# One burst of identity transposes in place of three, and two handovers made per token block

## The reference

```
i, f, g = x @ Wi.T, x @ Wf.T, x @ Wg.T
h[t] = sigmoid(f[t]) * h[t-1] + silu(i[t]) * (1 - sigmoid(f[t]))
xg = h * silu(g)
x1 = layernorm(x + (xg * rsqrt(mean(xg^2) + eps) * w_norm) @ Wo)
x2 = layernorm(x1 + wkv(w, u, keys=x1, values=ctx))     # a recurrence over the tokens
x3 = layernorm(x2 + int8_mlp(x2))                       # quantised per token and per weight row
```

## Time and profile before

| | |
|---|---|
| median of 3 runs | 420.44 us (419.89 to 420.63) |
| time of the profiled execution | 419.63 us |
| its span, first to last instruction | 417.7 us |
| PE busy | 370.7 us (89%) |
| DVE busy | 362.9 us (87%) |
| ACT busy | 320.9 us (77%) |
| POOL busy | 232.9 us (56%) |
| mean granted TensorE clock | 0.983 of full speed |

### The profile page before, as it was taken

One profiled execution on the slowest core, in us unless ns is written; L12 is line 12 of the kernel. 1 busy time (PEld: TensorE's weight loads), 2 busy tenths in 40 slices (PEclk: granted clock), 3 DMA queues, 4 the chain that ended last, 5 costly groups with the idle time before them and its releaser, 6 DMA issues.

```text
span 417.7 us, 7901 instructions
## 1 busy us (share of the span) xinstructions
PE 370.7 (89%) x2756; PEld 290.5 (70%) x2778; DVE 362.9 (87%) x620; ACT 320.9 (77%) x422; POOL 232.9 (56%) x274
## 2 busy tenths in 40 slices
PE   7798899989898899999999999999999998486872
PEld 7797798769775778678866977597759774233331
DVE  3889899869677899989998999899989999998684
ACT  3778599597927899599958996899679976985671
POOL 1574573843526656674667557664767554645451
PEclk9999999999999999999999999999999999888997
DMA  7978356010200020301011020202030202000101
GB/s 246 369 262 322 101 192 240 0 52 27 102 1 2 0 77 1 116 14 50 27 55 73 10 69 25 102 0 75 0 126 0 75 0 75 25 1 2 50 27 51
DMA packets 12842, 31.74 MB, mean 76 GB/s; under 512 B 2038, under 2 KB 5132, under 8 KB 12812
## 3 DMA queue, kind: packets, MB, share of 16 engines
q1 hardware_dynamic: 12812, 31.35, 21.5%
HBM read 27.14 MB, written 4.21 MB: 75 GB/s over the span
## 4 chain that ended last, share of the span: by engine, by line
DVE 26%; PE 24%; ACT 17%; issue 14%; POOL 14%; DMA 2%; SPq 1%; DVEq 0%; POOLq 0%; ACTq 0%
PE proj_ps L502 14%; PE slot_ps L607 6%; POOL den L1269 5%; ACT L1009 3%; DVE hid_top L1648 2%; DVE stats L1584 2%; ACT hqT L974 2%; DVE inp L1487 2%; POOL ring L1294 2%; DVE num L1577 2%; DVE ring L1629 2%; DMA ring<-w_gate_up_dram 2%; DVE x_max L1603 2%; DVE ring L1632 2%; POOL late L1299 2%
## 5 line engine op out<-in xcount | busy, mean ns | idle before, releaser
L1294 POOL TENSOR_TENSOR ring<-ring 128x512 f32<-128x512 f32 (+1 forms) x48 | 62.4, 1302 | 41.2 <-ACT ring L960 41.2
L607 PE MATMUL slot_ps<-w1q,xqT 128*128 128x512 bf16 (+1 forms) x377 | 80.0, 361 | 5.7 <-ACT xqT L951 2.9
L607 PEld LDWEIGHTS slot_ps<-w1q,xqT 128*128 128x128 bf16 x384 | 35.9, 98 | 44.6 <-issue 3.3
L502 PE MATMUL proj_ps<-x_high,proj_high 128*128 128x256 f32 x384 | 64.8, 290 | 0.9 <-ACT proj_high L887 0.5
L502 PE MATMUL proj_ps<-x_low,proj_high 128*128 128x256 f32 x384 | 61.6, 282 | 0.0
L502 PE MATMUL proj_ps<-x_high,proj_low 128*128 128x256 f32 x384 | 61.5, 282 | 0.0
L502 PEld LDWEIGHTS proj_ps<-x_high,proj_high 128*128 128x128 f32 x384 | 53.1, 189 | 2.9 <-issue 0.7
L502 PEld LDWEIGHTS proj_ps<-x_high,proj_low 128*128 128x128 f32 x384 | 52.7, 189 | 0.0
L502 PEld LDWEIGHTS proj_ps<-x_low,proj_high 128*128 128x128 f32 x384 | 52.4, 188 | 0.0
L960 ACT ACTIVATE ring<-ring,zero_bias,x_scale 128x512 f32<-128x512 f32 (+1 forms) x48 | 36.8, 771 | 15.6 <-DVE ring L1629 15.6
L1269 POOL TENSOR_TENSOR den<-den,q_state 128x512 f32<-128x512 f32 x16 | 28.1, 1771 | 35.2 <-ACT q_state L920 35.2
(11 more groups left out here) (146 smaller groups left out, 824.7 us busy)
## 6 DMA issues: line engine op xcount, KB each, us to landing
ring<-w_gate_up_dram SPq DMA_DIRECT2D x11, 512.0 KB, 4.4
forget<-xT_dram SPq DMA_DIRECT2D x8, 512.0 KB, 3.8
x_sb<-x_dram SPq DMA_DIRECT2D x8, 512.0 KB, 3.5
c_sb<-cT_dram SPq DMA_DIRECT2D x8, 512.0 KB, 4.4
out_dram<-late SPq DMA_DIRECT2D x16, 256.0 KB, 2.1
late<-w_down_dram SPq DMA_DIRECT2D x2, 704.0 KB, 6.7
ring<-w_down_dram SPq DMA_DIRECT2D x2, 704.0 KB, 4.4
scale_rows<-scratch_dram SPq DMA_DIRECT2D x2, 704.0 KB, 6.1
```

Of the source, the lines that this page charges most:

```text
L502: last = nc.tensor.matmul(out, a, b, start=(i == 0), stop=(i == len(terms) - 1))
L607: last = nc.tensor.matmul(slot_ps[:, s, half * 512:half * 512 + width], xqT[:, par, d, t * P:(t + 1) * P], w1q[:, d, half * I + at:half * ...
L1294: nc.gpsimd.tensor_tensor(hid, hid, gate_buf[:, at:at + width], ALU.mult).then_inc(hid_ready, 1)
```

## The change

In PE's prologue the three bursts and their three waits are replaced by one wait for `mlp_read` at 3 and one burst of 32 transposes; they write another place in PSUM. `split_states` subtracts one token block at a time, each with its own increment of `xg_low_ready`, and `project_out(b, t)` waits for its own block. `turn_inputs` goes through the token blocks in its outer loop and waits for `x2_rounded` of each block; it issues the same 8 transposes. The last two edits hold for every batch.

```diff
@@ project_out
                 pe.wait_ge(xg_high_ready, b + 1)
-                pe.wait_ge(xg_low_ready, b + 1)
+                pe.wait_ge(xg_low_ready, b * TB + t + 1)
@@ turn_inputs
-                pe.wait_ge(x2_rounded, 2 * b + 2)
                 pe.wait_ge(z2_ready, 2 * b + 2)
-                for c in range(DB):
-                    for t in range(TB):
+                for t in range(TB):
+                    pe.wait_ge(x2_rounded, 2 * b + t + 1)
+                    for c in range(DB):
                         last = nc.tensor.transpose(turn_16[:, c, t * P:(t + 1) * P],
                                                    low_halves(z2[:, t, c * P:(c + 1) * P]),
                                                    identity16[:, :])
@@ PE's list, prologue
             project(2, 5)
-            pe.wait_ge(proj_read, 2 * PROJ + 5)
-            keep_busy(28, proj_ps[:, 0, 0:P // 2])
-            pe.wait_ge(num_ready, 4)
-            keep_busy(36, proj_ps[:, 0, 0:P // 2])
-            pe.wait_ge(h_ready, 3)
-            keep_busy(28, proj_ps[:, 0, 0:P // 2])
+            pe.wait_ge(mlp_read, 3)
+            keep_busy(32)
             turn_values(1, 0)
@@ split_states on DVE
                 dve.wait_ge(xg_high_ready, b + 1)
-                nc.vector.tensor_tensor(flat(xg_low), flat(inp), flat(xg_high).bitcast(F32),
-                                        ALU.subtract).then_inc(xg_low_ready, 1)
+                for t in range(TB):
+                    tok = slice(t * P, (t + 1) * P)
+                    nc.vector.tensor_tensor(xg_low[:, :, tok], inp[:, :, tok],
+                                            xg_high[:, :, tok].bitcast(F32),
+                                            ALU.subtract).then_inc(xg_low_ready, 1)
```

## The result

The kernel after takes 418.22 us (median of 7 runs, 417.13 to 419.14), the kernel before on the same chip 420.70 (7 runs, 419.89 to 423.44). The ratio is 0.9921, 95% interval 0.9897 to 0.9946: faster by 3.3 us, between 2.3 and 4.3. The two medians themselves lie 2.5 us apart, which is inside that interval. 417.6 was forecast. Each interval here leaves out runs more than 1.5% above the fastest of their kernel, one of them a run of 750.10 us among the 12 of the kernel before that e5 to e8 are compared with.

What follows compares the result with a forecast made beforehand. No engine is full (PE 89%, DVE 87%), so the chain of waits decides, with late filler on it. Terms -3.26 + 0.25 + 0.45 + 0.05 - 0.35 = -2.86 from 420.44 give 417.6 us, range 415.8 to 418.7.

Steps and rivals of the forecast that it cites:

- The burst, -3.26: PE's prologue: 32 transposes end before refine's release, so hidden_max_row(0, 0) starts 3.26 us earlier, at 115.6.
- Batch 1, +0.45: Prologue: POOL's round_rows(12) steps between the halves of split_states(1), the second ends 1.5 us later, 0.45 reaches the chain.
- the lower bound of 0.05: Batch 1 in the prologue: the cost is only 0.05 us if DVE keeps its turn for both halves.
- `split_states` in the iterations, +0.25: Two DVE instructions of 0.6 us for one at 1.15 cost 0.05 us a batch, 0.25 over five.
- rival D: Slower: POOL's pair_squares steps between the split_states halves every iteration, +3.6 us, 424.0; chance 0.04.
- Batch 0, +0.05: split_states of batch 0, now in two halves, costs 0.05 us.
- `turn_inputs`, -0.35: Iterations: fewer transposes after the last round_2, but x1 limits the gain to 0.07 us on average, 0.35 over five.
- the bound of 1.15: Largest gain allowed for turn_inputs: the full 0.23 us in each of five iterations, 1.15 us.
- B: Engines don't take turns as read and x1 is no limit: -4.6 us, 415.9, or 416.7 with half the difference; chance 0.25.
- C: Most of the gain is hidden by another prologue wait late after 115: 419.7 us; chance 0.07.
- that the change doesn't do what it says: In PE's prologue, mlp_read is met later than read from the trace; no size given; chance 0.02.
- E: Slower: 60 transposes fewer let the granted clock fall after 110, 425.8 us; chance 0.04.

Runs made afterwards that it cites:

- e5: The kernel after without the burst of 32 and its wait: 418.28 us, 0.9931 of the kernel before.
- e8: The kernel after, with DVE in batch 1 alone waiting for its own first half of split_states before the second: 418.43 us, one run.
- e3: The kernel before with only split_states and its wait by token block: 421.31 us, 0.9992 of the kernel before.
- e4: The kernel before with only turn_inputs by token block: 419.05 us, 0.9924 of the kernel before.
- e1: The kernel before with only the new burst (wait for mlp_read at 3, 32 transposes): 418.17 us, 0.9913 of the kernel before.
- e12: The kernel after with an unused two-input POOL product added ahead of round_rows(12): 416.37 us, one run.
- e7: The kernel after with layer_norm_2(1) put ahead of split_states(2) and hidden_max_row(0, 0) on DVE: 417.16 us, 0.9914 of the kernel before.
- e11: The kernel after with DVE order layer_norm_2(1), first half of split_states(2), hidden_max_row(0, 0), second half: 415.21 us, 0.9839 of the kernel before.

## Why the prediction was right

The forecast was 417.6 and the measurement 418.22; the interval of the difference (-2.3 to -4.3) holds the -2.86 of the sum. Its terms did not all hold, and that it came so close to the medians (2.5 apart) is partly luck: the stages give -4.0, and the runs can't tell the two apart.

- **The burst, -3.26: right, by its own steps.** 32 transposes end ahead of `refine`, `residual_2` follows `gating(2)`, and POOL's third product is what is late next, lengthened to 1.5 us. Measured: -3.31. The third MLP chunk was forecast for 122.1 after waiting 1.6 us for DVE. It starts at 125.39, which is 122.1 and the 3.3 by which this execution is late, and waits 1.15. That the new wait holds nothing up is right too: the burst stands directly behind `project(2, 5)`.
- **Batch 1, +0.45: wrong.** The step that failed is "POOL gets its turn between two DVE instructions in a row". It had been read from a POOL product with two inputs and was carried over to a scaling with one. `normalise_2(0)` came 10.11 us after `gating(1)`, before 10.13. What happened is what the lower bound of 0.05 stands for: DVE keeps its turn for both halves.
- **`split_states` in the iterations, +0.25: right,** +0.27 (e3). All 16 halves on line 1490, by duration in ns (least, median, most), show that POOL never came between those of the iterations, which was rival D:

```profile
L1490 DVE TENSOR_TENSOR xg_low<-inp,xg_high x16: 673/684/692, 39.0 to 338.9; 128x512 fp32r<-128x512 f32 x16
```

- **Batch 0, +0.05:** +0.08, within the scatter: e4, which leaves `split_states` alone, shows +0.05 in the same stage.
- **`turn_inputs`, -0.35: right in its mechanism, mis-sized by a factor of three.** Measured -1.05 (e4), close to the bound of 1.15. In e4 every iteration is shorter by 0.19 to 0.23, iteration 1 included. The prediction let x1 stop the gain there, as x1 stood behind the load of x^T: "that path does not move". The rows after the change, to be set against the earlier trace rows:

```profile
174.63 0.38 PE L580 MATMUL turn_ps<-identity,num 128*128 128x128 f16 x4 [0.51 <-ACT num L940]
...
175.25 0.40 PE L580 MATMUL turn_ps<-identity,num 128*128 128x128 f16 x4 [0.23 <-ACT num L940]
...
175.68 1.11 ACT L947 ACTIVATE xqT<-turn_ps,half_bias 128x1024 bf16<-128x1024 f16 x1 [0.49 <-PE turn_ps L580]
...
177.18 1.15 ACT L862 ACTIVATE x_high<-forget,zero_bias 128x1024 fp32r<-128x1024 f32 x1 [0.38 <-DMA forget<-xT_dram]
178.23 1.51 ACT L928 ACTIVATE x<-inp,shift,rstd 128x512 f32<-128x512 f32 x2
...
180.40 1.04 PE L560 MATMUL turn_ps<-identity,x 128*128 128x128 f32 x8
```

  x1 is ready at 179.74, 0.61 earlier than before, because the load took 3.3 us from issue to landing and not 4.1. That was a matter of the execution: in e1 and e3, where `turn_inputs` is as before, ACT doesn't wait for this load at all. Nor did x1 hold `turn_keys` up. Counted from ACT's read of `xqT`, x1 is ready after 4.54 us in the profile before, 3.79 in e1, 3.73 in e3 and 4.06 after the change; the transposes of `turn_keys` start after 4.78, 4.72, 4.71 and 4.72. So they start when PE is through with the first two chunks of `mlp_up`, and the late x1 of the one profile before cost them 0.06. First PE's row of the kernel before, then e1's timelines:

```profile
180.59 1.06 PE L560 MATMUL turn_ps<-identity,x 128*128 128x128 f32 x8
```
```profile
173.28 1.11 ACT L947 ACTIVATE xqT<-turn_ps,half_bias 128x1024 bf16<-128x1024 f16 x1 [0.71 <-PE turn_ps L580]
174.51 1.15 ACT L862 ACTIVATE x_high<-forget,zero_bias 128x1024 fp32r<-128x1024 f32 x1
175.56 1.51 ACT L928 ACTIVATE x<-inp,shift,rstd 128x512 f32<-128x512 f32 x2
```
```profile
178.00 1.04 PE L560 MATMUL turn_ps<-identity,x 128*128 128x128 f32 x8
```

  The prediction took a distance of 0.21 us between x1 and the weight load, seen in one execution, for a dependence that limits.

The two wrong terms, +0.45 and -0.35, missed on the same side, by 0.45 and 0.70; with them put right the sum is -4.0, as the stages have it. The forecast stood because the burst's term, the largest, was right.

Of the rivals, B was half right (x1 was no limit) and half wrong (the engines do take turns: 1.52 at 117.33). C is refuted by the stage's -3.31, D by the halves above, and that the change doesn't do what it says by the burst's place. E, the lower clock after 110, did not occur in the profile after the change (1.00 from 110 to 118). It occurred in e4, with all the old bursts in place: the filler behind the pause did not prevent it.

## What to carry to other kernels

Filler on an in-order queue is free only up to the moment at which its successor could start: compare its end with the release of the next instruction, and place it before the pause, not behind the wait that ends the pause. Whether it is needed at all is a question of its own; here one profile without it kept the clock. When a wait is taken away, look at what is late next and at the order of that engine's list. Here one reordering on DVE gave another 1.4 us. And compare stages that repeat from execution to execution where totals spread by more than the effect looked for. A limit read from one execution is checked against a second one: here one slow load passed for the limit of an iteration.

## What the runs showed of the hardware

- A POOL instruction that meets two DVE subtractions back to back steps in between them if it multiplies two SBUF tensors (POOL 1.60 in e12 and 1.68 in e7, the DVE pair 2.37 and 2.35 instead of 1.27). If it scales one tensor by a column it waits for both (2.33, the pair 1.27; with 512 elements 2.64), unless DVE pauses for a semaphore between them (1.83, the pair 2.55). Between a scan and a DVE instruction with two tensors and a column the scaling steps in too (2.75, DVE 1.11 instead of 0.74). The Trainium skill (SBUF — State Buffer, section "SBUF: two separate sides") speaks of an exclusive lock on the shared ports. That one engine waits while the other runs agrees with all of these; which engine gets its turn next, these runs alone show.
- The same pause of PE, behind the same code, lowers the granted clock in one execution and not in another. Ahead of the old bursts, 1.95 us: 0.51 to 0.64 in e4, 1.00 in the kernel before. In the first 20 us, 2.04 in e5: down to 0.50; 2.00 in the kernel before: 1.00. Near 47 us, 1.81: 0.64 to 0.80 from 46 to 52 in e8 and e11, 1.00 after the change; the stage from `gating(0)` to `gating(1)` took 1.6 longer in these two. And 2.40 in e5, ahead of `turn_values`: 1.00. For e5, PE's timeline and a window:

```profile
18.21 0.62 PE L661 MATMUL slot_ps<-identity,ring 128*128 128x128 f16 x8 [2.04 <-POOL ring L1224]
```
```profile
20.00:22.00 2.00, 2.00 (x12) 2.00 (x11) 1.74 (x4) 2.00 (x3) 1.48 (x2) 0.50 0.93 305
```

- The start also depends on when weights land. After the change ACT waited 3.15 us for the weights of i, and PE 3.78 behind it:

```profile
16.32 1.15 ACT L883 ACTIVATE proj_high<-den,zero_bias 128x1024 fp32r<-128x1024 f32 x1 [3.15 <-DMA den<-wiT_dram]
```

  The change touches nothing there, and in the kernel before ACT's step began at 14.89. Late weights and the lower clock together put `gating(0)` at 36.53 instead of 33.27. By an estimate from these rows about half of that is the clock: PE went on 1.74 later (20.08 against 18.34) and `gating(0)` came 3.26 later; in e5 PE went on 0.13 earlier and `gating(0)` came 1.36 later. A spread of one to three us in the start is the reason why single executions can't rank kernels that differ by less.
